# Second attention walks its keys from the back, spreads the score tiles for the maxima evenly, and masks them on VectorE and GpSimd instead of TensorE

## The chip, the cores and the metric

The kernel runs on one core of one Trainium2 chip. The metric is the device time of one execution in microseconds (us), the median of several runs. An engine is named as the profile names it: PE is TensorE (PEld its weight loads), DVE is VectorE, ACT is ScalarE, POOL is GpSimd, SP is SyncE.

## What is computed

Two transformer-like layers on x of shape (2, 1024, 128) in float32. Layer 0 is a latent attention with 8 heads and a mixture of experts. Layer 1, where the change is, is causal attention with 16 heads of width 8, then a second mixture of experts. The part that matters:

```
def _L1_attn_ref(x, w_qkv, w_out):
    qkv = x @ w_qkv
    q, k, v = jnp.split(qkv, 3, axis=-1)
    ...                                   # 16 heads of width 8, rotary embedding on q and k
    scores = jnp.einsum('bhqd,bhkd->bhqk', q, k) * scale
    causal = jnp.tril(jnp.ones((S, S), dtype=bool))
    scores = jnp.where(causal, scores, jnp.finfo(scores.dtype).min)
    attn = jax.nn.softmax(scores, axis=-1)
    out = jnp.einsum('bhqk,bhkd->bhqd', attn, v)
    out = out.transpose(0, 2, 1, 3).reshape(B, S, D)
    return out @ w_out
```

## The kernel before

Every engine has one program in order, written out by hand, and they wait for each other by semaphores. The second attention is cut into eight units (`U1 = 8`): a unit is one batch and four heads (`HG = 4`), with its 1024 queries in two chunks of 512 and its keys in eight tiles of 128.

Scores are computed twice. Once as queries x keys, in `scores_max1` (L1331), to find each query's maximum over its keys: 40 pieces a unit, listed in `MX1`, each of one or two matmuls (L1348) into one bank of PSUM, out of which DVE reduces the maximum in `maximum1` (L2021). On the diagonal a mask of large negative numbers is added by a further matmul of 128 columns for each tile (`mask_qk`, L1352). A second time as keys x queries, in `scores1` (L1374), with the maximum as an extra row of the operand: ten steps a unit (`K1 = 10`), listed in `ST1`, each of one key tile (or two that share a bank) for four heads in four banks. ACT takes the exponential in `exps1` (L851, two heads at a time), and `values1` (L1400) multiplies by the values. Here too the causal mask is a matmul of 128 columns (`masks1`, L1386), ahead of the exponential. All of these run through the same PE.

The maxima belong to the unit after: while PE runs the ten steps of unit u, it weaves in the 40 pieces of unit u+1, five in each of steps 0 to 7 and none in 8 and 9 (`MX1_STEP`, function `piece` in `unit1`). The pieces have two PSUM banks (0 and 1), so piece n waits until DVE has reduced piece n-2 (`max1_done`). In step k, `values1` of step k-1 is issued behind the scores and three of the pieces of step k. After the last piece DVE splits the maxima into two parts (`split_max1`), PE turns them (`turn_max1`, L1361), ACT copies them (`max_rows1`), and the next unit's `scores1` can begin. The stacked queries and keys of the units ahead are staged by POOL (`stage`), turned by PE (`turn_stack`, L1327) and copied by ACT (`stack`, L613) through bank 7, which the turned contexts (`turn_context1`, L1408, read by `contexts_out1` on DVE) share. Of unit 0 the 40 pieces run ahead of the units, among the preparation of the second batch, with six banks. Units 2 to 5 run in a hardware loop of two units.

The four score banks hold step k+1's scores once ACT has taken step k's exponentials (`exp1_done`).

## Time and profile before

| | |
|---|---|
| median of 3 runs | 993.67 us (993.42 to 994.7) |
| profiled execution | 993.18 us, span of its instructions 991.3 us |
| PE, PEld busy | 849.9 us (86%), 505.0 us (51%) |
| DVE, ACT, POOL busy | 595.4 (60%), 516.4 (52%), 329.3 us (33%) |
| second attention, maxima of unit 0 | 559 to 616 us of the span |
| second attention, the eight units | 621 to 939 us of the span |

Busy time is what an engine spent on instructions. A PE matmul's row lasts longer than the room it takes in PE's stream, since matmuls overlap: the room is read from one start to the next. "Idle before, releaser" tells what an engine waited for ahead of an instruction. PEclk is the clock that TensorE was granted, where 1.00 is 2.4 GHz.

### The profile page before, as it was taken

How to read it: one execution, taken by the hardware profiler on the slowest of the kernel's cores; microseconds unless marked ns; L12 is line 12 of the kernel's file. 1: busy time of each engine (PE TensorE's matmuls, PEld its weight loads, DVE VectorE, ACT ScalarE, POOL GpSimd, SP SyncE). 2: the span in 40 equal slices, each digit the busy share in tenths (PEclk: the TensorE clock that was granted, in tenths of full speed). 3: DMA queues.
4: the chain of work that ended last, by engine and by line, in shares of the span. 5: the costliest groups of instructions: out<-in, count | busy, mean ns of one | idle time of the engine just before them, and what ended most of it. 6: DMA issues, size and time to landing. Idle time of an engine off the chain costs nothing.

```text
span 991.3 us, 15069 instructions
## 1 busy us (share of the span) xinstructions
PE 849.9 (86%) x5146; PEld 505.0 (51%) x5146; DVE 595.4 (60%) x1294; ACT 516.4 (52%) x875; POOL 329.3 (33%) x332
## 2 busy tenths in 40 slices
PE   5899999988999865899998435899999999999858
PEld 2454444343343233479987323555555555555435
DVE  6867776767666157553357598557575575754051
ACT  3246566564565642336665211656656566565632
POOL 3327666655566861660140840110202102000000
PEclk9779999998999996799999566899999999999969
DMA  9300000000000000112230200000000000000001
GB/s 330 123 1 1 1 1 1 1 1 1 1 1 1 1 1 0 59 59 62 70 97 29 84 3 1 1 1 1 1 2 1 1 0 0 0 1 1 1 1 43
DMA packets 22634, 24.38 MB, mean 25 GB/s; under 512 B 3591, under 2 KB 20105, under 8 KB 22314
## 3 DMA queue, kind: packets, MB, share of 16 engines
q1 hardware_dynamic: 19896, 17.90, 5.5%
q0 software_dynamic: 2048, 4.20, 1.5%
q10 hardware_dynamic: 626, 1.43, 0.4%
q8 instruction: 40, 0.66, 0.3%
q14 instruction: 24, 0.20, 0.1%
HBM read 14.34 MB, written 9.18 MB: 24 GB/s over the span
## 4 chain that ended last, share of the span: by engine, by line
PE 62%; DVE 23%; ACT 7%; issue 5%; POOL 2%; DMA 1%; ACTq 0%; DVEq 0%; SPq 0%; POOLq 0%
PE ps L1348 8%; PE ps L1400 6%; PE ps L1032 6%; PE ps L1024 5%; PE ps L1001 5%; DVE mx_part L2021 5%; PE ps L1374 4%; DVE mx_part L1631 3%; ACT rounded L613 3%; PE ps L1040 3%; PE ps L1291 3%; DVE cT L1654 2%; PE ps L990 2%; PE ps L1202 2%; ACT pt L851 2%
## 5 line engine op out<-in xcount | busy, mean ns | idle before, releaser
L1631 DVE TENSOR_REDUCE mx_part<-ps 128x1 f32<-128x512 f32 x256 | 162.5, 681 | 70.6 <-PE ps L1001 69.8
L851 ACT ACTIVATE pt<-ps 128x1024 f32<-128x1024 f32 (+1 forms) x160 | 142.8, 938 | 86.7 <-PE ps L1374 45.7
L670 ACT ACTIVATE pt<-ps 128x512 f32<-128x512 f32 x256 | 139.9, 596 | 80.3 <-PE ps L1024 78.2
L2021 DVE TENSOR_REDUCE mx_part<-ps 128x1 f32<-128x512 f32 (+3 forms) x256 | 138.9, 586 | 37.7 <-PE ps L1352 23.9
L1348 PE MATMUL ps<-rounded 128*128 128x512 f32 (+3 forms) x384 | 143.1, 426 | 12.2 <-DVE mx_part L2021 4.5
L613 ACT ACTIVATE rounded<-ps 32x512 fp32r<-32x512 f32 (+3 forms) x166 | 98.2, 593 | 100.9 <-PE ps L1327 32.2
L1024 PE MATMUL ps<-rounded 100*128 100x512 f32 x256 | 121.0, 484 | 8.5 <-ACT pt L670 7.8
L1001 PE MATMUL ps<-rounded 98*128 98x512 f32 x256 | 107.9, 444 | 17.4 <-DVE mx_part L1631 16.7
L1348 PEld LDWEIGHTS ps<-rounded 128*128 128x128 f32 x384 | 73.7, 203 | 76.2 <-DVE mx_part L2021 49.8
L1374 PE MATMUL ps<-rounded 128*128 128x512 f32 (+3 forms) x384 | 104.2, 370 | 8.9 <-ACT pt L851 7.2
L2021 DVE TENSOR_REDUCE mx<-ps 128x1 f32<-128x128 f32 (+3 forms) x128 | 57.2, 487 | 83.4 <-PE ps L1352 82.0
L490 POOL TENSOR_TENSOR xnT<-pt 128x512 f32<-128x512 f32 x64 | 80.9, 1282 | 72.6 <-ACT pt L670 71.9
L490 POOL TENSOR_TENSOR xn<-pt 128x512 f32<-128x512 f32 x64 | 80.3, 1283 | 59.2 <-ACT pt L670 55.5
L1024 PEld LDWEIGHTS ps<-rounded 100*128 100x128 f32 x256 | 48.1, 191 | 78.8 <-ACT pt L670 46.7
L577 POOL COPY v_cur<-early 128x288 f32 (+1 forms) x8 | 3.4, 425 | 221.6 <-PE ps L1400 221.6
L1400 PE MATMUL ps<-pt,v_cur 128*9 128x512 f32 (+3 forms) x768 | 76.9, 488 | 0.1
L1032 PE MATMUL ps<-pt,ckv 128*32 128x512 f32 x512 | 74.8, 659 | 0.9 <-ACT pt L670 0.9
L1001 PEld LDWEIGHTS ps<-rounded 98*128 98x128 f32 x256 | 50.8, 201 | 47.7 <-issue 29.9
L1374 PEld LDWEIGHTS ps<-rounded 128*128 128x128 f32 x384 | 60.7, 191 | 24.0 <-ACT pt L851 17.0
L1987 DVE TENSOR_TENSOR pt<-ps,pt 128x352 f32<-128x352 f32 x46 | 24.1, 523 | 52.2 <-ACT pt L797 52.2
L1654 DVE RECIPROCAL cT<-ps 128x128 f32<-128x128 f32 x32 | 29.5, 936 | 39.1 <-PE ps L1040 39.1
L613 ACT ACTIVATE pt<-ps 128x128 f32<-128x128 f32 (+2 forms) x96 | 37.6, 393 | 25.6 <-PE ps L1283 14.4
(249 smaller groups left out, 1285.9 us busy)
## 6 DMA issues: line engine op xcount, KB each, us to landing
wm<-in_wm SPq DMA_DIRECT2D x1, 4896.0 KB, 15.5
kstage<-to_experts SPq DMA_DIRECT2D x10, 256.0 KB, 3.4
of_experts<-pt SPq DMA_DIRECT2D x10, 256.0 KB, 2.3
to_experts<-kstage SPq DMA_DIRECT2D x4, 512.0 KB, 4.1
wm<-in_experts SPq DMA_DIRECT2D x1, 1028.0 KB
x<-in_x SPq DMA_DIRECT2D x4, 256.0 KB, 6.2
out<-x SPq DMA_DIRECT2D x4, 256.0 KB, 2.3
to_experts<-kstage SPq DMA_DIRECT2D x2, 448.0 KB, 4.4
```

The costliest lines, as they stand in the source:

```text
L490: nc.gpsimd.tensor_tensor(pair_sum[j % 2][i], pt0(0, i), pt0(1, i), ALU.add).then_inc(pair_add, 1)
L613: return nc.scalar.activation(dst, src, ACT.Copy)
L670: nc.scalar.activation(pt0(k, i), ps[:, ST0_BANKS[i % 2], :], ACT.Exp, scale=SCALE0).then_inc(exp_done, 1)
L851: nc.scalar.activation(pt[:, 4 * (t % 2) + 2 * g:4 * (t % 2) + 2 * g + 2, 0:w], ps[:, ST1_BANKS[2 * g]:ST1_BANKS[2 * g] + 2, 0:w], ACT.Exp ...
L1001: mm(ps[:, max_bank(u, n), :], cq[0:NZ, b * S + j * P:b * S + (j + 1) * P], key_stack[u % 2][0:NZ, h, c * CH:(c + 1) * CH], start=True, st ...
L1024: mm(ps[:, ST0_BANKS[i % 2], :], key_stack[pp][0:NZM, h, k * P:(k + 1) * P], query_stack[pp][0:NZM, h, c * CH:(c + 1) * CH], start=True, s ...
L1032: ins = mm(ps[ctx_rows(pp, i), CTX_BANK, :], ckv[:, k, u // UH, :], pt0(k, i), start=(k == 0), stop=(k == TS - 1))
L1348: ins = mm(bank[:, o:o + w], query_stack1[pp][:, i * P:(i + 1) * P], key_stack1[pp][:, r, c * CH:c * CH + w], start=(o == 0), stop=not diag)
L1374: ins = mm(ps[:, ST1_BANKS[r], o:o + w], key_stack1[pp][:, r, j * P:(j + 1) * P], query_stack1[pp][:, q0:q0 + w], start=(o == 0), stop=not ...
L1400: ins = mm(ps[RS * r:RS * r + DH + 1, CTX_BANK, CH - w:CH], v_cur[pp][:, j, r, :], pt[:, 4 * (t % 2) + r, o:o + w], start=(j == 0), stop=( ...
L1631: v.tensor_reduce(mx_part[u % 2][:, o:o + 1], ps[:, max_bank(u, n), :], AX_X, ALU.max).then_inc(max_done, 1)
L2021: v.tensor_reduce(dst, ps[:, banks[s % len(banks)], o:o + w], AX_X, ALU.max).then_inc(max1_done, 1)
```

## The change

1. `ST1` is turned round: the second chunk of queries comes first, then the first, and in each the diagonal key tiles first and then the others from the back. `MX1` is turned round as well (second half of queries on the second half of keys, then on the first half, then the first half), with the pieces of one head side by side.
2. Four pieces in each of the ten steps, one behind each head's scores, in place of five in eight. The stream of pieces runs eight ahead (`MX1_AHEAD`): steps 8 and 9 of unit u hold the first eight pieces of unit u+2, and eight pieces of unit 1 stand ahead of unit 0.
3. No mask matmuls. For the maxima, DVE adds a mask tile `later` in SBUF and takes the maximum in one `tensor_tensor_reduce`, which writes the sum back to PSUM; it is two instructions on the engine. For the exponentials, POOL sets the forbidden ones to zero behind ACT (`mask`, `affine_select` on a block of 4 x 128 columns, eight blocks a unit), and `values1` of a diagonal step waits for POOL (`masked1`) in place of ACT.
4. The last step's values go into the next unit's step 0; the copies of keys by ACT are spread one by one behind the exponentials (`STACK1_KEYS`); POOL stages keys before queries, in separate functions; all eight units are written out, without the loop.

The core of the diff:

```
-for c in range(S // CH):
+for c in reversed(range(S // CH)):
     j0 = c * TC
-    ST1 += [(c, ((j, 0, CH),)) for j in range(j0 + 1)]
-    ST1 += [(c, ((j0 + 1, 0, CH - P), (j0 + 3, CH - P, P))), (c, ((j0 + 2, 0, CH - 2 * P),))]
+    own = [(c, ((j0, 0, CH),)), (c, ((j0 + 1, 0, CH - P), (j0 + 3, CH - P, P))), (c, ((j0 + 2, 0, CH - 2 * P),))]
+    ST1 += own + [(c, ((j, 0, CH),)) for j in reversed(range(j0))]
...
-    MX1 += [(r, c, p) for p in parts for r in range(HG)]
+    MX1 += [(r, c, p) for r in range(HG) for p in parts]
...
-MX1_STEP = (5, 5, 5, 5, 5, 5, 5, 5, 0, 0)
+MX1_AHEAD = 2 * HG
...
+            def mask(u, k):
+                if DIAG1[k]:
+                    pool.wait_ge(exp1_done, u * (2 * K1) + (2 * k + 2))
+                for o, w in DIAG1[k]:
+                    block = pt[:, 4 * (k % 2):4 * (k % 2) + HG, o:o + P]
+                    nc.gpsimd.affine_select(block, block, [[0, HG], [1, P]], ALU.is_ge, 0.0, base=0,
+                                            channel_multiplier=-1).then_inc(masked1, 1)
...
                 for i, o, w in parts:
-                    diag = c == i // TC
                     ins = mm(bank[:, o:o + w], query_stack1[pp][:, i * P:(i + 1) * P],
-                             key_stack1[pp][:, r, c * CH:c * CH + w], start=(o == 0), stop=not diag)
-                if diag:
-                    for i, o, w in parts:
-                        ins = mm(bank[:, o + w - P:o + w], identb[:], mask_qk[:], start=False,
-                                 stop=(o == parts[-1][1]))
+                             key_stack1[pp][:, r, c * CH:c * CH + w], start=(o == 0), stop=(o == parts[-1][1]))
...
-                pe.wait_ge(exp1_done, u * (2 * K1) + (2 * t + 2))
+                if DIAG1[t]:
+                    pe.wait_ge(masked1, u * NDIAG1 + DIAG1_UPTO[t])
+                else:
+                    pe.wait_ge(exp1_done, u * (2 * K1) + (2 * t + 2))
...
                 for k in range(K1):
-                    scores1(u, pp, 0, k, first)
-                    scores1(u, pp, 1, k, first)
-                    piece(k, 0)
-                    scores1(u, pp, 2, k, first)
-                    scores1(u, pp, 3, k, first)
-                    piece(k, 1)
-                    masks1(k)
-                    piece(k, 2)
+                    for r in range(HG):
+                        scores1(u, pp, r, k, first)
+                        piece(k, r)
...
+            for n in range(MX1_AHEAD):
+                scores_max1(1, 1, n)
+            for u in range(U1):
+                unit1(u, u % 2, first=(u == 0), s=(u + 1 < U1), t=(u + 2 < U1))
...
-                    v.tensor_reduce(dst, ps[:, banks[s % len(banks)], o:o + w], AX_X, ALU.max).then_inc(max1_done, 1)
+                    tile = ps[:, banks[s % len(banks)], o:o + w]
+                    if c == i // TC:
+                        v.tensor_tensor_reduce(tile, tile, later[:, CH - w:CH], 1.0, NEG, ALU.add, ALU.max,
+                                               dst).then_inc(max1_done, 1)
+                    else:
+                        v.tensor_reduce(dst, tile, AX_X, ALU.max).then_inc(max1_done, 1)
```

PE, steps 8 and 9 of a unit before, from the last head's scores of step 8 on. L1374 are scores, L1386 their masks, L1400 values, L1361 turned maxima; there is no piece in them:

```order
L1374 MATMUL ps<-rounded 128x384
L1374 MATMUL ps<-rounded 128x128
L1386 MATMUL ps<-mask_kq,identb 128x128 x8
L1400 MATMUL ps<-pt,v_cur 9x512 x4
L1361 MATMUL ps<-identr,qstage 128x128 x4
L1374 MATMUL ps<-rounded 128x256 x4
L1386 MATMUL ps<-mask_kq,identb 128x128 x4
L1400 MATMUL ps<-pt,v_cur 9x384 x4
L1400 MATMUL ps<-pt,v_cur 9x128 x4
L1361 MATMUL ps<-identr,qstage 128x128 x4
```

PE in step 8 now, from the second head on (L1403 are scores, L1382 pieces, L1420 values, L1428 turned contexts):

```order
L1403 MATMUL ps<-rounded 128x384
L1403 MATMUL ps<-rounded 128x128
L1382 MATMUL ps<-rounded 128x256
L1403 MATMUL ps<-rounded 128x384
L1403 MATMUL ps<-rounded 128x128
L1382 MATMUL ps<-rounded 128x512
L1403 MATMUL ps<-rounded 128x384
L1403 MATMUL ps<-rounded 128x128
L1382 MATMUL ps<-rounded 128x128
L1382 MATMUL ps<-rounded 128x384
L1420 MATMUL ps<-pt,v_cur 9x512 x4
L1428 MATMUL ps<-ident,cT 128x128 x4
```

What moved: the masks are gone, and a piece stands behind each head's scores.

DVE, a stretch of a unit before: one instruction for each tile, whether masked or not (register operations of the loop between them), and then a context:

```order
L2021 TENSOR_REDUCE mx_part<-ps 128x1
L2017 REGISTER_ALU
L2021 TENSOR_REDUCE mx_part<-ps 128x1
L2038 ISA
L2041 RECIPROCAL rden<-ps 128x16
L2042 ISA
L2045 ISA
L2045 TENSOR_TENSOR half<-ps,rden 128x4x32
```

DVE over the masked tiles of steps 7 to 9 now (ISA is the masked maximum and, behind it, the instruction that hands out its result):

```order
L2043 ISA ps,mx_part<-ps,later 128x128
L2043 ISA mx_part 128x1
L2043 ISA ps,mx_part<-ps,later 128x384
L2043 ISA mx_part 128x1
L2067 RECIPROCAL rden<-ps 128x16
L2071 TENSOR_TENSOR half<-ps,rden 128x4x32
L2043 ISA ps,mx_part<-ps,later 128x256
L2043 ISA mx_part 128x1
L2043 ISA ps,mx_part<-ps,later 128x512
L2043 ISA mx_part 128x1
```

What moved: a masked tile is a pair, and the masked tiles of the next unit but one stand on both sides of the context.

PE between the last piece of unit 0 and the scores of unit 0, before:

```order
L1361 MATMUL ps<-identr,qstage 128x128 x8
L1327 MATMUL ps<-identr,qstage 128x128 x4
L1327 MATMUL ps<-identr,kstage 128x128 x4
L1374 MATMUL ps<-rounded 128x512 x2
L1348 MATMUL ps<-rounded 128x128
L1348 MATMUL ps<-rounded 128x384
```

The same place now (L1391 turned maxima, L1363 turned stacks):

```order
L1391 MATMUL ps<-identr,qstage 128x128 x4
L1363 MATMUL ps<-identr,qstage 128x128 x4
L1391 MATMUL ps<-identr,qstage 128x128 x4
L1382 MATMUL ps<-rounded 128x128
L1382 MATMUL ps<-rounded 128x384
L1382 MATMUL ps<-rounded 128x256
L1382 MATMUL ps<-rounded 128x512
...
L1403 MATMUL ps<-rounded 128x512
```

What moved: three groups of transposes in place of four, and eight pieces that stood in unit 0's steps before.

## Rows read from the trace of the kernel before

**Rows 1.** The page: busy times, and the chain that ended last.
```profile
PE 849.9 (86%) x5146; PEld 505.0 (51%) x5146; DVE 595.4 (60%) x1294; ACT 516.4 (52%) x875; POOL 329.3 (33%) x332
...
PE 62%; DVE 23%; ACT 7%; issue 5%; POOL 2%; DMA 1%; ACTq 0%; DVEq 0%; SPq 0%; POOLq 0%
```

**Rows 2.** Timeline, POOL: start us, us, instruction; the copy that ends each unit.
```profile
666.20 0.42 POOL L577 COPY v_cur<-early 128x288 f32 x1 [42.34 <-PE ps L1400]
...
748.57 0.42 POOL L577 COPY v_cur<-early 128x288 f32 x1 [35.80 <-PE ps L1400]
...
872.48 0.43 POOL L577 COPY v_cur<-early 128x288 f32 x1 [35.98 <-PE ps L1400]
```

**Rows 3.** Windows (start:end, length, busy PE, PEld, DVE, ACT, POOL, clock, DMA): one unit; unit 0's maxima.
```profile
748.58:789.87 41.29, 39.16 (x289) 23.39 (x289) 25.97 (x55) 26.00 (x35) 5.00 (x11) 1.00 0.01 1
...
560.00:585.00 25.00, 10.86 (x41) 7.54 (x41) 23.61 (x56) 0.60 (x1) 18.23 (x22) 0.57 0.09 24
```

**Rows 4.** Waits in that unit: who waited for whom, us, times, longest.
```profile
PEld ps L1348 <- DVE mx_part L2021: 7.2, 12, 1.0
...
PEld ps L1348 <- DVE mx L2021: 1.4, 3, 0.9
```

**Rows 5.** Timeline, PE, in and around that unit.
```profile
742.18 0.62 PE L1386 MATMUL ps<-mask_kq,identb 128*128 128x128 bf16 x8
742.73 1.05 PE L1400 MATMUL ps<-pt,v_cur 128*9 128x512 f32 x8
...
761.26 0.71 PE L1374 MATMUL ps<-rounded 128*128 128x512 f32 x2
...
765.04 0.63 PE L1374 MATMUL ps<-rounded 128*128 128x512 f32 x2
...
782.31 1.33 PE L1374 MATMUL ps<-rounded 128*128 128x384 f32 x8
```

**Rows 6.** Groups by form: busy, mean ns.
```profile
L2021 DVE TENSOR_REDUCE mx_part<-ps 128x1 f32<-128x512 f32 x160 | 103.8, 686 | 21.6 <-PE ps L1348 13.2 <-PE ps L1352 8.2
...
L1352 PE MATMUL ps<-mask_qk,identb 128*128 128x128 bf16 x256 | 50.1, 238 | 0.0
...
L1386 PE MATMUL ps<-mask_kq,identb 128*128 128x128 bf16 x256 | 22.6, 221 | 0.0
...
L2021 DVE TENSOR_REDUCE mx_part<-ps 128x1 f32<-128x128 f32 x32 | 9.2, 286 | 7.5 <-PE ps L1352 7.2
```

**Rows 7.** Timeline, DVE: short instructions, free ones and two that depend.
```profile
592.55 0.37 DVE L1929 BATCH_NORM_AGGREGATE mv<-stats 128x2 f32<-128x6 f32 x4
...
593.84 0.16 DVE L1947 TENSOR_TENSOR norm<-norm 128x4 f32<-128x4 f32 x1
594.03 0.16 DVE L1949 SCALAR_TENSOR_TENSOR norm<-norm 128x4 f32<-128x4 f32 x1
```

**Rows 8.** Groups by form: an addition on DVE from PSUM and SBUF, and one from two of SBUF.
```profile
L1918 DVE SCALAR_TENSOR_TENSOR x<-xnT,share,x 128x128 f32<-128x128 f32 x32 | 8.7, 346 | 0.0
...
L1749 DVE TENSOR_TENSOR x<-ps,x 128x512 f32<-128x512 f32 x4 | 2.7, 674 | 0.0
```

**Rows 9.** Groups of POOL and ACT.
```profile
L490 POOL TENSOR_TENSOR xnT<-pt 128x512 f32<-128x512 f32 x64 | 80.9, 1282 | 72.6 <-ACT pt L670 71.9
...
L468 POOL TENSOR_SCALAR xn<-x,mv,lnv 128x128 f32<-128x128 f32 x8 | 6.3, 789 | 1.4 <-DVE lnv L1579 1.4
...
L566 POOL COPY xn<-big 128x256 f32 x12 | 4.8, 400 | 39.3 <-PE ps L1361 38.0 <-POOL kstage L574 1.0
```

**Rows 10.** Timeline, PE: first pieces of unit 0, the turned maxima, first scores, and unit 7's.
```profile
558.96 0.90 PE L1348 MATMUL ps<-rounded 128*128 128x128 f32 x2 [2.48 <-ACT rounded L613]
...
616.41 0.75 PE L1361 MATMUL ps<-identr,qstage 128*128 128x128 f32 x4 [6.47 <-DVE qstage L2034]
...
621.40 1.18 PE L1374 MATMUL ps<-rounded 128*128 128x512 f32 x2
...
911.82 1.21 PE L1374 MATMUL ps<-rounded 128*128 128x512 f32 x4
```

More of the change, by code:

```diff
@@ L125 @@
 MX1 = []
-for i0, c in ((0, 0), (TC, 0), (TC, 1)):
+for i0, c in ((TC, 1), (TC, 0), (0, 0)):
     if c * TC == i0:
@@ new lines, in exps1 @@
+            def exps1(u, t, g, first):
+                w = sum(m for _, _, m in ST1[t][1])
+                act.wait_ge(st1_mm, u * (2 * K1) + (2 * t + g + 1))
+                if not (first and t < 2):
+                    act.wait_ge(pv1_mm, u * K1 + (t - 1))
+                nc.scalar.activation(pt[:, 4 * (t % 2) + 2 * g:4 * (t % 2) + 2 * g + 2, 0:w],
+                                     ps[:, ST1_BANKS[2 * g]:ST1_BANKS[2 * g] + 2, 0:w], ACT.Exp,
+                                     scale=SCALE1).then_inc(exp1_done, 1)
@@ L874, in _ @@
+                    if k == 0 and not first:
+                        context1_T(u - 1, 1)
+                    if k == K1_FIRST:
+                        context1_T(u, 0)
             act.wait_ge(keys_zero[0], 1)
-            for n in range(4):
-                stack(0, 0, n)
+            for n in range(2):
+                for r in range(HG):
+                    stack_keys(0, 0, n, r)
+                stack_queries(0, 0, n)
             for c in range(NCH // B, NCH):
@@ L1426, in unit1 @@
                     if k:
                         values1(u, pp, k - 1, first)
-                    for n in range(3, max(MX1_STEP)):
-                        piece(k, n)
-                    if s and k in STACK1_SECOND:
-                        n = 2 + STACK1_SECOND.index(k)
-                        turn_stack(u + 1, 1 - pp, n, (stacked, u * 4 + (n + 4)))
-                    if k == CTX1_BEFORE and not first:
-                        turn_context1(u - 1, 1, (stacked, u * 4 + 8) if s else (m1_rows, u * 2 + 2))
@@ L2072, in _ @@
             split_max1(0, 0)
-            unit1(0, 0, first=True)
-            unit1(1, 1)
-            with dve.Fori(1, U1 // 2 - 1) as i:
-                unit1(i * 2, 0)
-                unit1(i * 2 + 1, 1)
-            unit1(U1 - 2, 0)
-            unit1(U1 - 1, 1, s=False)
+            for n in range(MX1_AHEAD):
+                maximum1(1, 1, n)
+            for u in range(U1):
+                unit1(u, u % 2, s=(u + 1 < U1), t=(u + 2 < U1))
             contexts_out1(U1 - 1, 1)
```

324 lines of the change are left out of this document (169 added, 155 removed).

## The prediction, made before the changed kernel was run

> **What bounds the kernel now.** I read the page first. PE is busy for 86% of the span, holds 62% of the chain that ended last, and DVE holds 23% of it [rows 1]. That is an average over stages, so the next view is the stage that the change touches. The copy of the values by POOL stands at the end of each unit; from 666.20 to 872.48 us there are five units of 41.3 us each [rows 2]. The windows show one of them: in 41.29 us PE is busy for 39.16, DVE for 25.97 and ACT for 26.00, at a full clock of 1.00 [rows 3]. So the five units, unit 6 (872.48 to 911.82, 39.3 us) and unit 7 (about 26.8 us, without pieces) [rows 2, 10] are PE's.
>
> PE's 39.16 us are not all work. A matmul that waits for a semaphore also shows its weight load late, and the waits say that the loads of the pieces stood for 7.2 + 1.4 us behind DVE's maxima in that unit [rows 4]. The two banks of the pieces tie PE to DVE: five pieces in a step are some 3.3 us for DVE at 0.69 us each [rows 6], and a step without any mask takes 3.78 us (761.26 to 765.04) [rows 5]. Steps 8 and 9, in which DVE has nothing, take 7.6 us (782.31 to the end of the unit at 789.87) [rows 3, 5].
>
> The stage ahead is another one. While the maxima of unit 0 are taken, DVE is busy for 23.61 of 25 us and PE for 10.86, at a granted clock of 0.57, near the lower of its two levels (1.2 of 2.4 GHz) [rows 3]. There DVE is the bound, from the first pieces at 558.96 to the split maxima at 616.41 [rows 10].
>
> **The masks that PE loses.** 256 + 256 mask matmuls [rows 6] are 64 a unit. Their rows of 0.22 to 0.24 us overlap; eight in a line took from 742.18 to 742.73, 0.069 us each [rows 5]. That is 64 x 0.069 = 4.4 us of PE's stream a unit, and 41.3 - 4.4 = 36.9 us if every wait stays as it is. It can be less: a mask in front of a wait for DVE only filled that wait.
>
> **What DVE gets.** A unit has 32 masked tiles (four heads, two diagonal chunks, four tiles each), and on each the reduction becomes an addition with maximum and a second instruction. A reduction costs 0.286 us for 128 columns and 0.686 for 512, so 1.04 ns a column and 0.15 us fixed [rows 6]. An addition of PSUM and SBUF of 512 columns took 0.674 us [rows 8], so the first of the pair costs no more than the reduction did, if it runs a column at a time. The trace has no such pair. For the second, the nearest rows are short instructions on a few columns: free ones start 0.07 us apart ((0.37 - 0.16) / 3), dependent ones 0.19 [rows 7]. I take 0.09, near the free ones, as nothing stands between the two, and keep 0.05 to 0.25. DVE then has 25.97 + 32 x 0.09 = 28.9 us a unit (27.6 to 34). Four masked pieces are 4/3 of a head's 1.94 + 4 x 0.09 = 2.30, so 3.1 us a step; four plain ones 2.7 us.
>
> The Trainium skill, "VectorE: DVE Perf Modes", section on two Vector instructions with no wait between them, says that an operation which writes out its accumulator is two instructions, and that one is held until all earlier ones end only if its start quadrants differ. Here all start in partition 0, so by the page the second is not held; the free rows 0.07 us apart agree.
>
> **Four pieces in every step.** The plain step of 3.78 us loses one piece, some 0.35 us, to 3.4. Ten such are 34 us, and the turned tiles (eight groups of four a unit, some 0.37 us of room each) bring 2.9: 36.9 us again. Two short steps of 256 columns take off 0.8. Against it stand the waits which the new order makes. In step 8 the turned context must be read by DVE before the turned maxima may use the bank: DVE waits for PE there, 0.5 us. The split of the maxima stands behind the last piece of step 7, three dependent instructions, 0.6 us, ahead of step 8's pieces. Together 37.2 us a unit with the POOL wait below at nothing; DVE's 3.1 us in masked steps hide behind the 3.4. I keep 35.0 to 40.0.
>
> **POOL's masks.** Eight blocks of 4 x 128 columns a unit, one in four steps and two in two. The values of step k stand behind the scores and pieces of step k+1, so that after the second exponential PE still has two heads' scores and two pieces, about 1.6 us, ahead of them. No row shows the operation. A copy of 256 columns took 0.400 us, an addition of 512 took 1.282, and an operation with two scalars of 128 columns 0.789 [rows 9]: for 512 columns 0.8, 1.3 and 3.2 us. I take the middle, 1.3 us or less: one block is covered, two (2.6 us) are late by up to 1 us, in which DVE works off its two banks. POOL has time: 5.00 us busy in 41.29 [rows 3]. Its own staging of keys comes ahead of the mask of step 0, 2.4 us of the 3.2 before that exponential ends.
>
> **ACT** keeps its 26.00 us [rows 3]; with a context and two copies in step 0 it has 3.7 us there, once, covered by the scores' banks. Its exponentials in diagonal steps start earlier by PE's masks.
>
> **The start.** DVE-bound, so 32 pairs cost 32 x 0.09 = 2.9 us. Keys are staged, turned and copied before queries, which lets the first piece start 1.8 us earlier. Then eight pieces of unit 1 (two thirds of a unit's 2.30 x 4, 6.1 us for DVE) stand on PE ahead of the first scores: 616.41 moves to 617.5, three groups of transposes as close as before end near 621, the last piece is issued about 5 us later, scores at 626 instead of 621.40 [rows 10]. Unit 0 took 44.8 us from there to 666.20 [rows 2, 10], with stalls at its start that are now gone. With 37.2 + 1 for the table of the exponential it ends at 664.4: 1.8 us won, start and unit 0 together.
>
> **The sum.** Units 1 to 5: 5 x (41.3 - 37.2) = 20.5. Start and unit 0: 1.8. Unit 6 has no pieces in steps 8 and 9, 37.2 - 1.8 = 35.4 against 39.3: 3.9. Unit 7: 12 + 12 + 8 masks less on PE, but its values now wait for POOL with no pieces for cover: nothing, within 3 us. Unrolling: nothing; the other stages are written out as well. Total 26.2 us. The profiled execution took 993.18 us, 1.9 more than its span, and 0.5 less than the median: 993.7 - 26.2 = 967.5, so 968 us.
>
> **Rivals.**
>
> *PE's masks had filled waits.* For it: the pieces' 8.6 us behind DVE [rows 4]. Against it: in steps 8 and 9 no piece is there to wait. Only the 32 masks of the scores would count (2.2 us) less what new waits cost (0.9), so 40 us a unit: 7 x 1.3 less 1 at the start, about 985 us.
>
> *The spread frees more.* If the 8.6 us behind DVE shrink by half, a unit is 35.0 us, near PE's own work: 6 x 2.2 + 3 more than forecast, about 952 us.
>
> *The masked maximum takes two cycles a column (slower).* It reads and writes the same bank of PSUM column by column, which no row of before does. 10,240 masked columns a unit x 1.04 ns = 10.7 us on DVE: 39.6 us, plus its waits for contexts and split and the gap behind the values, 2.5 to 4, is 43 us. DVE is then the bound: 7 x 43 against 7 x 41.3, with the start (DVE-bound, 10.7 + 2.9 and the eight pieces 9 us) about +30, 1023 us. It decides from 26.2 / 256 = 0.10 us more for each of the 8 x 32 masked tiles than I take, if all of it lands on the path. Against it: 0.674 us for 512 columns of an addition that reads PSUM and writes elsewhere [rows 8].
>
> The Trainium skill, "Vector Engine (DVE) Microarchitecture Reference", section on points that are easy to get wrong, states that the scalar-tensor-tensor form with two sources in SBUF that are not bf16 halves throughput. Here one source is PSUM, so by the page it does not apply; the trace's own addition of that form from two float32 tiles of SBUF, 0.346 us for 128 columns [rows 8], shows no doubling either, without an accumulator.
>
> *POOL's masks are slow (slower).* At 2.5 us a block, single blocks are 0.9 us late and double ones 3.4: 4 x 0.9 + 2 x 3.4 = 10.4 us a unit on PE, less 3 of slack: 44.6 us, about 1025 us. It decides from 1.7 us a block.
>
> **How the numbers follow.** Forecast 0.42 (959 to 977), filled waits 0.17, more freed 0.13, the costs and gains cancel 0.05, slow maximum 0.13, slow POOL 0.10. Faster by over 0.2% (2 us, what this measurement can tell): 0.72. Same: 0.05. Slower: 0.23. The range reaches to the rival of 952 below, and above to 1004, beyond the upper bound of the second instruction: 0.16 us more on 256 tiles are 41 us, less 0.3 us of slack in six steps of seven units, 12.6, which gives 996: some 0.06 lie below and 0.14 above.
>
> **What would show it.** Units 37.2 us apart by the copies of the values; DVE busy 28 to 30 us in each, the pair's second instruction under 0.1 us from start to start; POOL's block at 1.3 us or less, with the values waiting for it only after the double blocks; DVE idle in no step for more than 1.5 us; first scores near 626 us, at the start. It is wrong if DVE has no idle time in masked steps, if values wait for POOL in single ones, or if the clock of 1.00 in the units falls as PE waits more.

## The result, and the profile after

| | before | changed |
|---|---|---|
| median of the runs | 993.54 us (4 runs) | 949.74 us (947.73 to 950.35, 4 runs) |
| ratio, 95% interval | | 0.9554, 0.9537 to 0.9571 |
| span of the profiled execution | 991.3 us | 948.6 us |

The kernel is 4.5% faster. The forecast was 968 us, 2.6% faster, in a range from 951 to 1004: the direction held, the gain was 44 us instead of 26, and the time fell 1.3 us below the range.

Page of the changed kernel, busy times and chain, against [rows 1]:

```profile
PE 814.8 (86%) x4634; PEld 478.3 (50%) x4634; DVE 605.9 (64%) x1550; ACT 518.4 (55%) x875; POOL 368.2 (39%) x396
...
PE 62%; DVE 27%; ACT 5%; issue 4%; POOL 2%; DMA 1%; ACTq 0%; SPq 0%; DVEq 0%; POOLq 0%
```

PE lost its 512 mask matmuls and 35 us of busy time. The shares of the chain hardly moved: which engine holds it says nothing of how much shorter it is. Timeline of POOL, the copies that mark the units, against [rows 2]:

```profile
706.55 0.43 POOL L588 COPY v_cur<-early 128x288 f32<-128x288 f32 x1
742.70 0.43 POOL L588 COPY v_cur<-early 128x288 f32<-128x288 f32 x1
```

A unit takes 36.15 us instead of 41.3. Its window and its waits, against [rows 3, 4]:

```profile
706.55:742.70 36.15, 34.74 (x226) 19.65 (x224) 27.77 (x88) 26.23 (x35) 9.95 (x20) 1.00 0.00 1
```

```profile
DVE ps L2043 <- PE ps L1382: 4.4, 8, 1.1
...
DVE mx_part L2046 <- PE ps L1382: 2.2, 3, 0.9
PEld ps L1382 <- DVE mx_part L2046: 2.2, 6, 0.5
PEld ps L1382 <- DVE mx L2043: 1.8, 4, 0.7
```

PE's busy time fell from 39.16 to 34.74, by 4.42 us, which looks like the 64 x 0.069 us of the prediction but isn't the masks alone (see e18 and e19); its idle time fell from 2.13 to 1.41. The pieces' weight loads wait for DVE for 5.0 us in all (a third row of 1.0 us, for the masked partial maxima, beside the two shown) instead of 8.6, and DVE itself waits 6.6 us for pieces.

Where the 42.7 us of span went, by the starts of the units' scores in both traces:

| stretch | before | after | won | forecast |
|---|---|---|---|---|
| start to first scores, and unit 0 | 621.40 + 44.8 | 621.27 + 36.6 | 8.3 | 1.8 |
| units 1 to 5 | 5 x 41.3 | 5 x 36.13 | 25.8 | 20.5 |
| unit 6 | 39.3 | 33.7 | 5.6 | 3.9 |
| unit 7 | 27.4 | 25.2 | 2.2 | 0 |
| behind it | 52.0 | 51.2 | 0.9 | 0 |

The first row is a sum of four: the start stage begins 1.6 us later in the trace of the changed kernel (its memset on DVE at 547.07 instead of 545.46 us), is 6.5 us shorter, is followed by 4.7 us more between the split maxima and the first scores, and unit 0 is 8.2 us shorter.

### The profile page after: what moved, and what is told of

The parts are those of the page before. It is cut to its first block, busy times and chain, and to the rows that moved or that the text cites. A ratio compares the mean times of both kernels' runs of the same rounds, so it can differ in the third digit from the quotient of the medians.

```text
span 948.6 us, 13753 instructions
## 1 busy us (share of the span) xinstructions
PE 814.8 (86%) x4634; PEld 478.3 (50%) x4634; DVE 605.9 (64%) x1550; ACT 518.4 (55%) x875; POOL 368.2 (39%) x396
## 4 chain that ended last, share of the span: by engine, by line
PE 62%; DVE 27%; ACT 5%; issue 4%; POOL 2%; DMA 1%; ACTq 0%; SPq 0%; DVEq 0%; POOLq 0%
PE ps L1382 7%; PE ps L1420 6%; PE ps L1068 6%; PE ps L1060 6%; DVE ps L2043 5%; PE ps L1403 5%; PE ps L1037 5%; DVE mx_part L1651 4%; PE ps L1076 3%; PE ps L1327 3%; DVE cT L1674 2%; PE ps L1238 2%; ACT rounded L645 2%; PE ps L1026 2%; PE ps L1309 2%
## 5 line engine op out<-in xcount | busy, mean ns | idle before, releaser
L1651 DVE TENSOR_REDUCE mx_part<-ps 128x1 f32<-128x512 f32 x256 | 162.4, 681 | 70.4 <-PE ps L1037 69.6
L882 ACT ACTIVATE pt<-ps 128x1024 f32<-128x1024 f32 (+1 forms) x160 | 148.9, 938 | 65.2 <-PE ps L1403 63.8
L1382 PE MATMUL ps<-rounded 128*128 128x512 f32 (+3 forms) x384 | 140.6, 410 | 11.6 <-DVE mx L2043 4.8
L2043 DVE CUSTOM_DVE_ANT_0 ps<-ps,later 128x128 f32<-128x128 f32 (+3 forms) x256 | 119.4, 519 | 45.6 <-PE ps L1382 44.8
L1060 PE MATMUL ps<-rounded 100*128 100x512 f32 x256 | 123.3, 493 | 8.5 <-ACT pt L702 7.9
L1403 PE MATMUL ps<-rounded 128*128 128x512 f32 (+3 forms) x384 | 124.0, 367 | 0.6 <-ACT pt L882 0.2
L1037 PE MATMUL ps<-rounded 98*128 98x512 f32 x256 | 106.0, 433 | 18.2 <-DVE mx_part L1651 17.3
L597 POOL TENSOR_SCALAR_AFFINE_SELECT pt<-pt 128x512 f32<-128x512 f32 x64 | 40.0, 637 | 207.9 <-ACT pt L882 207.9
L1382 PEld LDWEIGHTS ps<-rounded 128*128 128x128 f32 x384 | 74.2, 203 | 49.7 <-DVE mx L2043 15.5
L2046 DVE TENSOR_REDUCE mx_part<-ps 128x1 f32<-128x512 f32 x128 | 82.0, 686 | 16.3 <-PE ps L1382 16.0
L1403 PEld LDWEIGHTS ps<-rounded 128*128 128x128 f32 x384 | 69.4, 190 | 45.1 <-issue 21.2
L1060 PEld LDWEIGHTS ps<-rounded 100*128 100x128 f32 x256 | 49.3, 196 | 81.6 <-ACT pt L702 45.8
L1420 PE MATMUL ps<-pt,v_cur 128*9 128x512 f32 (+3 forms) x768 | 76.8, 488 | 1.5 <-POOL pt L597 1.5
L548 POOL DMA_INDIRECT xnT<-of_experts,slot_i x32 | 30.7, 960 | 57.1 <-DMA of_experts<-pt 47.8
```

Source lines behind the costliest of these rows:

```text
L882: nc.scalar.activation(pt[:, 4 * (t % 2) + 2 * g:4 * (t % 2) + 2 * g + 2, 0:w], ps[:, ST1_BANKS[2 * g]:ST1_BANKS[2 * g] + 2, 0:w], ACT.Exp ...
L1037: mm(ps[:, max_bank(u, n), :], cq[0:NZ, b * S + j * P:b * S + (j + 1) * P], key_stack[u % 2][0:NZ, h, c * CH:(c + 1) * CH], start=True, st ...
L1060: mm(ps[:, ST0_BANKS[i % 2], :], key_stack[pp][0:NZM, h, k * P:(k + 1) * P], query_stack[pp][0:NZM, h, c * CH:(c + 1) * CH], start=True, s ...
L1382: ins = mm(bank[:, o:o + w], query_stack1[pp][:, i * P:(i + 1) * P], key_stack1[pp][:, r, c * CH:c * CH + w], start=(o == 0), stop=(o == p ...
L1403: ins = mm(ps[:, ST1_BANKS[r], o:o + w], key_stack1[pp][:, r, j * P:(j + 1) * P], query_stack1[pp][:, q0:q0 + w], start=(o == 0), stop=(o ...
L1420: ins = mm(ps[RS * r:RS * r + DH + 1, CTX_BANK, CH - w:CH], v_cur[pp][:, j, r, :], pt[:, 4 * (t % 2) + r, o:o + w], start=(j == CTX1_START ...
```

## The experiments

Every ratio is to the kernel before, run on the same chip. Two groups of runs (e10 to e13, and e18 with e19; marked *) fell on chips on which the kernel before took 1034 us; in their traces the start stage begins 35 to 41 us later than in the others. Units are as long there as elsewhere (compare e10 with the changed kernel, e12 with e1). So most verdicts are read from the distance of two copies that mark a unit, which repeats within 0.1 us in one trace from unit 2 on, and from the way between two DVE instructions of the start stage: its memset and the first instruction of the split maxima. "Start" is that distance: 70.45 us before, 63.95 after. The starts marked * can't be compared with the others: in each of them DVE stands for 3 to 9 us in all at places where no trace of the other chips has waits of that length, whether the run moves the zeroing on GpSimd (e10 to e12) or not (e13, e18, e19). Why is open, and the kernel before has no trace from these chips.

| run | us | ratio (95%) | unit | start |
|---|---|---|---|---|
| changed kernel | 949.7 | 0.9554 (0.9537 to 0.9571) | 36.13 | 63.95 |
| e1 plain maxima | 942.8 | 0.9482 (0.9458 to 0.9507) | 35.37 | 63.1 |
| e3 one-column memset more | 948.4 | 0.9565 (0.9540 to 0.9589) | 36.12 | 63.9 |
| e13 96-column memset more | 1001.7 | 0.9708 (0.9664 to 0.9751) | 36.80 | 72.1* |
| e2 no GpSimd masks | 950.8 | 0.9568 (0.9541 to 0.9595) | 36.13 | 64.2 |
| e7 GpSimd's masks twice as long | 960.0 | 0.9668 (0.9640 to 0.9695) | 36.94 | 63.9 |
| e4 maxima's masks on PE | 964.5 | 0.9699 (0.9666 to 0.9731) | 37.12 | 69.2 |
| e17 scores' masks on PE | 956.8 | 0.9633 (0.9607 to 0.9660) | 37.08 | 64.0 |
| e18 both on PE | 1017.9 | 0.9840 (0.9804 to 0.9876) | 39.05 | 71.9* |
| e19 both, and five pieces | 1023.7 | 0.9906 (0.9871 to 0.9942) | 40.74 | 70.9* |
| e5 five pieces | 959.3 | 0.9665 (0.9632 to 0.9698) | 37.85 | 64.0 |
| e6 before, maxima's masks on DVE | 983.2 | 0.9910 (0.9880 to 0.9939) | 39.98 | 70.5 |
| e8 values in halves | 1022.7 | 1.0303 (1.0269 to 1.0337) | 45.00 | 64.0 |
| e10 zeroing late | 991.1 | 0.9611 (0.9565 to 0.9657) | 36.11 | 67.8* |
| e12 the same, plain maxima | 982.7 | 0.9526 (0.9483 to 0.9569) | 35.37 | 64.9* |
| e11 before, zeroing late | 1035.6 | 1.0031 (1.0002 to 1.0059) | 41.28 | 71.3* |
| e14 zeroing between | 948.9 | 0.9537 (0.9511 to 0.9563) | 36.13 | 61.3 |
| e15 before, zeroing between | 985.9 | 0.9918 (0.9891 to 0.9946) | 41.29 | 62.8 |
| e16 zeroing between, plain maxima | 939.9 | 0.9465 (0.9441 to 0.9488) | 35.38 | 60.3 |

### What the masked maximum costs: e1, e3, e13

DVE's timeline of the changed kernel, unit 0's first maxima:

```profile
559.48 0.60 DVE L2043 CUSTOM_DVE_ANT_0 ps<-ps,later 128x384 f32<-128x384 f32 x1
560.00 0.14 DVE L2043 DVE_READ_ACCUMULATOR2_ANT mx_part<- 128x1 f32 x1
560.00 0.47 DVE L2043 CUSTOM_DVE_ANT_0 ps<-ps,later 128x256 f32<-128x256 f32 x1
560.38 0.14 DVE L2043 DVE_READ_ACCUMULATOR2_ANT mx_part<- 128x1 f32 x1
560.38 0.73 DVE L2043 CUSTOM_DVE_ANT_0 ps<-ps,later 128x512 f32<-128x512 f32 x1
561.03 0.14 DVE L2043 DVE_READ_ACCUMULATOR2_ANT mx_part<- 128x1 f32 x1
561.03 0.33 DVE L2043 CUSTOM_DVE_ANT_0 ps<-ps,later 128x128 f32<-128x128 f32 x1
```

Read the starts, not the durations: the accumulator's read and the next main instruction start together. The four tiles of a head start 0.52 + 0.38 + 0.65 us and, from 561.03 to the next row, 0.25 us apart: 1.79 us a head.

```
- v.tensor_tensor_reduce(tile, tile, later[...], 1.0, NEG, ALU.add, ALU.max, dst)
+ v.tensor_reduce(dst, tile, AX_X, ALU.max)                       # e1
+ v.memset(x_lo[:, n:n + 1], 0.0)            # e3, behind each masked maximum
+ dve.wait_ge(max1_done, done); v.memset(x_lo[:, slot:slot + 96], 0.0)  # e13, the same place
```

> The changed kernel, with a plain maximum over the unmasked scores in place of the masked maximum in all 256 own-half tiles (32 in a unit; the causal mask of the maxima is left out). Theory A: the masked maximum costs no more than a plain one, since its second instruction (the read of the accumulator) lies under the start of the next one; then the time stays within 1.5 us of the changed kernel's 949.7 us. Rival B, the price of the prediction: 0.09 us for each second instruction, 2.9 us of VectorE a unit, of which TensorE waits for a part; then the time falls to between 930 and 945 us.

> The changed kernel with one more small VectorE instruction (a memset of one column, 128x1) behind each of the 256 masked maxima, which brings back the 0.09 us that the prediction charged for the second instruction, or somewhat less. VectorE gets 1.9 to 2.9 us a unit more. Theory A: VectorE stands idle for about 1 us in each step, at the values, and TensorE waits for it in the rest of the step, so that a third to a half comes through: 0.7 to 1.4 us a unit, 956 to 961 us. Rival B: all of it comes through, as VectorE is the bound within masked steps: 965 to 972 us. Rival C: the idle time takes it all: under 952 us.

> The changed kernel with a memset of 96 columns on VectorE behind each of the 256 masked maxima (some 0.08 us more of VectorE's stream each, by its memset of 4096 columns in 3.47 us, plus what it can't overlap), close to the 0.09 us of the prediction's step. With plain maxima 0.055 us less on 32 tiles gave 0.77 us a unit, so that 44% of VectorE's time came through. Theory A: the same share of 2.6 us: units 1.1 us longer, 37.3 us, and 2.5 us in the start stage: 960 us (956 to 963). Rival B: hidden like the memset of one column: 950 to 952. Rival C: all of it: units of 38.7 us, 970 us.

e1 gave 0.76 us a unit (and 0.9 in the start). Theory A, a pair no dearer than a plain maximum, falls by 5 us; 942.8 lies in B's band, but B's reason falls too, since the read has no time of its own in the rows above. Plain maxima of four tiles take 1.63 us back to back: e15 has 12 of them in one row.

```profile
561.02 4.88 DVE L2022 TENSOR_REDUCE mx<-ps 128x1 f32<-128x128 f32 x12 [11.20 <-PE ps L1353]
```

4.88 / 3 = 1.63 against 1.79: the main instruction costs 0.04 us a tile more than the reduction, 1.3 us a unit, the read nothing. Of these 1.3 us more than half (0.76) came through to the unit. The read is in time what the Trainium skill, "VectorE: DVE Perf Modes", section on two Vector instructions with no wait between them, calls not held; the prediction quoted it and still charged 0.09. A small instruction more (e3, rival C) costs nothing either: the unit stays at 36.12 us and the start at 63.9. e13's memset, which also has a wait on a semaphore ahead of it (for the tile before), does cost:

```profile
759.74 0.14 DVE L2048 MEMSET x_lo<- 128x96 f32 x1
759.80 0.54 DVE L2043 CUSTOM_DVE_ANT_0 ps<-ps,later 128x384 f32<-128x384 f32 x1
760.25 0.14 DVE L2043 DVE_READ_ACCUMULATOR2_ANT mx<- 128x1 f32 x1
760.35 0.14 DVE L2048 MEMSET x_lo<- 128x96 f32 x1
760.40 0.41 DVE L2043 CUSTOM_DVE_ANT_0 ps<-ps,later 128x256 f32<-128x256 f32 x1
```

A head now takes 759.43 to 761.75, 2.32 us, so memset and wait take 0.13 us more a tile and 4.2 us a unit; the unit became 0.67 us longer. One sixth came through, where A had said 44%; DVE's idle time in the unit fell from 8.4 to 6.5 us. By this run the predicted 0.09 us would have cost about 0.67 x 0.09 / 0.13 = 0.46 us a unit, an estimate; why e1 let through more than half and e13 a sixth is open. e13's total can't be read against the changed kernel's, since its start stage has a stand of its chip in it.

### What GpSimd's masks cost: e2, e7

```
- nc.gpsimd.affine_select(block, block, ...)         # e2: none
+ nc.gpsimd.affine_select(idle, idle, ...)           # e7: one more, ahead of each
```

> The changed kernel without the 64 instructions of GpSimd on the exponentials (the causal mask of the exponentials is left out); the values wait for the exponentials themselves. Theory A: the masks are hidden in units 0 to 6, and cost only the 1.5 us by which the values wait for GpSimd in unit 7: 948 us, between 947 and 949.5. Rival B: they also hold buffers and so hold back ScalarE and TensorE in every unit: under 945 us.

> The changed kernel with a second, idle GpSimd instruction of the same form and size ahead of each of the 64 masks of exponentials, so that a block takes about 1.3 us (the price that the prediction took) instead of 0.64, and a step with two blocks 2.5 us. Theory A: single blocks stay hidden, double blocks come up to 1 us late in each unit's two steps, at most 2 us a unit, and unit 7 pays 2 to 3 us: 953 to 966 us. Rival B: hidden in all units but the last: 951 to 953 us. Rival C: GpSimd becomes the bound with its staging behind the masks: over 970 us.

Groups by form of the changed kernel (busy us, mean ns), and two PE rows of unit 7:

```profile
L597 POOL TENSOR_SCALAR_AFFINE_SELECT pt<-pt 128x512 f32<-128x512 f32 x64 | 40.0, 637 | 207.9 <-ACT pt L882 207.9
```

```profile
878.58 1.05 PE L1420 MATMUL ps<-pt,v_cur 128*9 128x384 f32 x16 [0.79 <-POOL pt L597]
...
895.14 1.55 PE L1420 MATMUL ps<-pt,v_cur 128*9 128x384 f32 x24 [0.71 <-POOL pt L597]
```

A block is 0.64 us, half of the 1.3 taken. Without the masks (e2, whose exponentials stay unmasked) units are as long as with them; theory B falls, and the 1.5 us of unit 7 that the trace shows can't be told in the total (950.8, above theory A's 949.5). At 1.27 us a block (e7) a unit is 0.81 us longer. From values to values its steps are those of the changed kernel but for the two with double blocks, 0.3 and 0.5 us longer: single blocks stay hidden at the predicted price, double ones come up to 0.5 us late. The step of the prediction on POOL's cover held, and theory A; its price was double.

### What each part of the change is worth in a unit: e4, e17, e18, e5, e19, e6

```
+ mm(bank[:, o + w - P:o + w], identb[:], mask_qk[:], start=False, ...)     # e4, e18, e19
+ mm(ps[:, ST1_BANKS[r], o:o + P], identb[:], mask_kq[:], start=False, ...) # e17, e18, e19
- MX1_AHEAD = 2 * HG; piece n = HG * k + r + MX1_AHEAD
+ MX1_AHEAD = 0; five pieces in steps 0 to 7                                # e5, e19
```

> The changed kernel with the maxima's masks back on TensorE: 32 mask matmuls a unit and plain maxima; everything else (order, four pieces a step, GpSimd's masks of the exponentials) stays. Theory A: each mask matmul takes its 0.069 us of TensorE's stream, 2.2 us a unit, less the 0.77 us that plain maxima gave: units of 37.6 us instead of 36.13, 960 us in all (957 to 963). Rival B: the matmuls fill waits for VectorE: units under 36.7 us, 951 to 954 us.

> The changed kernel with the pieces spread as before: five in each of the steps 0 to 7 (the fifth behind the values), none in 8 and 9, and none ahead of a unit; no other change. Theory A: the spreading was worth what the waits for VectorE lost, 8.6 us of weight loads before against 5.0 after, of which the idle time of TensorE shows 0.7 us: units of 36.9 us, and the eight pieces ahead of unit 0's scores come back into the unit: 953 to 958 us. Rival B: all 3.6 us of the waits return: units near 39.7 us, 970 to 978 us. Rival C: the spread is worth nothing, units of 36.1 us, and the time is 948 to 951.

> The kernel before, with only the maxima's masks moved: masked maxima on VectorE, no mask matmuls in the 32 masked tiles of a unit (VectorE's program is unrolled for it); the masks of the scores stay on TensorE, five pieces a step. Theory A: TensorE loses 2.2 us a unit and the pair costs 0.8: units of 39.5 to 39.9 us instead of 41.3, 981 to 985 us. Rival B: the masks had filled waits for VectorE, which is slower now: 41.0 us or more, 991 us or above. Rival C: with the masks gone, waits shrink with them: under 39 us, below 978.

> The changed kernel with the masks of the scores back on TensorE (32 mask matmuls a unit, each behind its head's scores) and none by GpSimd. Theory A: they cost their stream, 32 x 0.055 to 0.069: units of 37.9 to 38.3 us instead of 36.13, and the parts add up: 36.13 + 2.0 + 1.0 (maxima's masks) + 1.7 (spread) = 40.8 of the 41.3 before; ratio to before 0.970. Rival B: they add more, 3 us a unit or above, since they lengthen ScalarE's way in the masked steps too: 0.977 or above. Rival C: under 1 us a unit: then the rest is the order's (keys from the back, copies by head).

> The changed kernel with both kinds of masks back on TensorE (64 mask matmuls a unit) and four pieces a step. Theory A: a mask alone fills waits for VectorE, two kinds do so less: more than the sum of the single runs, 36.13 + 2.5 to 3.5 = 38.6 to 39.6 us a unit. Rival B: they add up: 38.1 us a unit.

> As the run beside it, and with five pieces in steps 0 to 7 and none in 8 and 9: all that is left of the change is the order (keys from the back, maxima by head, copies by head, the places of the turned tiles) and the unrolling. Theory A: the order is worth nothing in a unit: 41.0 to 41.5 us, as before. Rival B: the order is worth the missing 1.5 us: 39.8 us a unit or less.

POOL's copies in e4, e17, e18, e19 and e5, each in its fence:

```profile
754.22 0.43 POOL L588 COPY v_cur<-early 128x288 f32<-128x288 f32 x1
791.37 0.42 POOL L588 COPY v_cur<-early 128x288 f32<-128x288 f32 x1
```

```profile
743.43 0.42 POOL L589 COPY v_cur<-early 128x288 f32<-128x288 f32 x1
780.51 0.42 POOL L589 COPY v_cur<-early 128x288 f32<-128x288 f32 x1
```

```profile
760.08 0.42 POOL L589 COPY v_cur<-early 128x288 f32<-128x288 f32 x1
799.11 0.43 POOL L589 COPY v_cur<-early 128x288 f32<-128x288 f32 x1
```

```profile
755.24 0.42 POOL L589 COPY v_cur<-early 128x288 f32<-128x288 f32 x1
795.96 0.42 POOL L589 COPY v_cur<-early 128x288 f32<-128x288 f32 x1
```

```profile
741.00 0.42 POOL L588 COPY v_cur<-early 128x288 f32<-128x288 f32 x1
778.83 0.43 POOL L588 COPY v_cur<-early 128x288 f32<-128x288 f32 x1
```

Undone one after the other from the changed kernel, the parts are worth: both kinds of masks 36.13 to 39.05 (2.9 us), the spread on top 39.05 to 40.74 (1.7), the order and unrolling that are left 40.74 to 41.3 (0.6). So 5.2 us are accounted for in full. With five pieces a step the masks are worth the same (e19 to e5, 40.74 to 37.85). Theory A of e19 (41.0 to 41.5) is missed by 0.3, B falls.

PE's busy time in a unit tells another sum. Windows of e18, e19 and e5:

```profile
760.08:799.11 39.03, 38.73 (x289) 22.84 (x289) 26.45 (x56) 26.50 (x35) 5.01 (x11) 1.00 0.01 2
```

```profile
755.24:795.96 40.72, 39.76 (x289) 22.90 (x288) 26.30 (x56) 26.39 (x35) 5.00 (x12) 1.00 0.00 1
```

```profile
741.00:778.83 37.83, 35.44 (x224) 19.37 (x224) 27.77 (x89) 26.32 (x35) 9.91 (x19) 1.00 0.00 1
```

The masks take 4.0 us of it at four pieces a step (38.73 to 34.74) and 4.3 at five (39.76 to 35.44), but a unit gets only 2.9 us shorter: PE's idle time grows by 1.1 and 1.4 us as they leave.

The two kinds of masks do not add up. Either kind alone costs 1.0 us (e4, e17), both 2.9 (e18: theory A), where their stream is 4.4. In e4 and e18 plain maxima give back e1's 0.76 us, so that the masks themselves cost 1.75 us of 2.2 in e4 and 3.7 of 4.4 in e18. The rest went into waits: the weight loads of the pieces stand for DVE for 5.0 us in a unit of the changed kernel, 3.8 in e17, 2.5 in e4 (4.1 in e1) and 2.6 in e18. So either kind fills waits for DVE, and behind the maxima's masks the others find no more of them. e17 meets its rival C (under 1 us a unit) by 0.05 us, its total lies between A and C, and what C concludes, that the rest is the order's, falls by e18 and e19. e4 lies between its theories A and B in a unit and came to 964.5 us by its start, below. The rival "PE's masks had filled waits" was right by a third. e6 agrees: from before, moving the maxima's masks alone gave 1.3 us of the 2.2 of their stream (theory A).

Waits of the pieces' weight loads in a unit of e5, then of e18:

```profile
PEld ps L1382 <- DVE mx L2040: 4.4, 7, 0.9
PEld ps L1382 <- DVE mx_part L2040: 3.6, 8, 0.9
PEld ps L1382 <- DVE mx_part L2043: 3.5, 9, 0.7
```

```profile
PEld ps L1380 <- DVE mx_part L2045: 2.2, 5, 0.5
PEld ps L1380 <- DVE mx L2045: 0.4, 1, 0.4
```

e5 shows the spread's 1.7 us in a unit, twice its theory A, with and without the masks (e19 against e18). These waits are what it takes away: 11.5 us in e5 against 5.0 with four pieces, 7.9 in e19 against 2.6. Its start is shorter by the eight pieces (first marking copy at 665.27 instead of 670.44), so the total lost 9.6 us and not 12.

### Values in halves: e8

```
- values1(k - 1), all heads, behind the fourth piece
+ values1(k - 1, heads 0, 1) behind the third, (heads 2, 3) behind the fourth
```

> The changed kernel with the values of a step in two halves (heads 0 and 1 behind the third piece, heads 2 and 3 behind the fourth) instead of one block behind the fourth, to close the 0.6 to 1.1 us in which VectorE has no piece in each step. Theory A: VectorE gets its pieces evenly, the 5.0 us for which TensorE's weight loads wait for it in a unit shrink to 2 or 3, and TensorE's idle 1.4 us go to 0.7: units of 35.4 us, 944 us (942 to 947). Rival B: TensorE's own stream is the bound and its idle time is elsewhere: no change, 948 to 951. Rival C: the first half waits for ScalarE or GpSimd, having one head of scores and a piece less ahead of it: units over 36.5 us, 953 us or more.

The time is 73 us longer. It lies in rival C's open band (953 us or more), but not for its reason: in a unit the values' weight loads wait 0.2 us for ScalarE and never for GpSimd. All three theories fall. Timeline of PE in e8, then in the changed kernel:

```profile
693.63 1.03 PE L1421 MATMUL ps<-pt,v_cur 128*9 128x512 f32 x4
694.59 0.50 PE L1403 MATMUL ps<-rounded 128*128 128x512 f32 x1
```

```profile
710.64 1.05 PE L1420 MATMUL ps<-pt,v_cur 128*9 128x512 f32 x8
711.61 0.50 PE L1403 MATMUL ps<-rounded 128*128 128x512 f32 x1
```

Eight matmuls of four heads and four matmuls of two heads hold PE for 0.97 and 0.96 us until the next scores start: the four heads, whose results go to four separate quarters of the partitions, run side by side, and half of them take as long as all. In each of the ten steps the second half costs what the whole did, 0.97 us, or 0.55 in the two steps of 256 columns: 8.9 us, and a unit grew by 8.87.

### The start stage: e10, e11, e12, then e14, e15, e16

Timeline of DVE and POOL in the start stage, of the kernel before, then of the changed one:

```profile
570.08 3.53 POOL L593 MEMSET rounded<- 128x4096 f32 x1
...
570.98 4.43 DVE L1927 COPY norm<-stats 128x4 f32<-128x4 f32 x1
...
577.38 0.65 DVE L1947 TENSOR_TENSOR norm<-norm 128x4 f32<-128x4 f32 x1
```

```profile
571.68 3.53 POOL L614 MEMSET rounded<- 128x4096 f32 x1
...
572.73 5.03 DVE L1978 TENSOR_SCALAR xn<-x,mv,norm 128x128 f32<-128x128 f32 x4
```

Before, the norm's chain of small instructions begins beside POOL's memsets: its head stands for 4.4 us until they end, and those behind it run beside POOL's staging at 0.16 to 0.65 us each. After, the chain is done 3 us earlier against POOL's clock and only its last step meets the memsets. e4 puts the masks back, its first mix comes 0.8 us later, and the whole collision returns (start 69.2 us). The first try moved the memsets behind the chain, the second ahead of it:

```
+ pool.wait_ge(max1_done, MX1_END[SECOND_ADD[0] + 1])   # e10, e11, e12: ahead of the memsets
- gather(1); memsets
+ first half of gather(1); memsets; second half           # e14, e15, e16
```

> The changed kernel with GpSimd's zeroing of unit 1's tiles in the start stage held until VectorE has taken the first maximum behind the first mix. In the changed kernel the copy of the normalized rows (VectorE) took 5.03 us beside these memsets and 1.12 us in its second place. Theory A: VectorE's copy cannot run beside GpSimd's memsets; free of them it gives back up to 3.9 us: from VectorE's own memset to the split maxima 60.0 us instead of 63.9, 946 us in all (944 to 948). Rival B: what holds the copy is something else (its own data): 949 to 951. Rival C: the memsets now collide with the second mix or hold up the staging of unit 1, and nothing is won or up to 3 us lost.

> The kernel before with the same delay of GpSimd's zeroing. There the blocked instruction is the copy at the head of the norm's chain (4.43 us instead of 0.17), and the 12 small instructions behind it ran beside GpSimd's staging (0.16 to 0.65 us each). Theory A: both go: 4.1 and about 3 us, from VectorE's memset to the split maxima 63.5 us instead of 70.45: 986 us (984 to 988), and half of what the change won in the start stage was that its chain of small instructions came ahead of the memsets. Rival B: only the blocked copy: 989 us. Rival C: no change, 993.

> The changed kernel with plain maxima (the causal mask of the maxima left out) and with GpSimd's zeroing held as in the run beside it. Theory A: the two gains are in different places (0.77 us a unit, and 3.9 us in the start stage) and add up: 939 us (937 to 941). Rival B: in the start stage they overlap: 942 to 943.

In e10, e11 and e12 the memsets lay beside plain maxima and cost nothing, but POOL's staging behind them (619.93 to 625.35 us in e10) met the second mix (as rival C of e10 had it):

```profile
620.20 4.86 DVE L1939 SCALAR_TENSOR_TENSOR x<-xnT,share,x 128x128 f32<-128x128 f32 x8
```

It takes 2.18 us undisturbed. The Trainium skill, "SBUF — State Buffer", section on its two separate sides, has a rule that sorts these rows: GpSimd shares a port pair, one at a time, with DVE instructions in a two-port mode, and with those that have two sources in SBUF only where GpSimd's instruction reads SBUF. The traces agree: a copy of one source stood beside a memset (4.43 us), a mix of two sources beside copies and additions (4.86), and reductions from PSUM beside neither. That the copy ran in a two-port mode no row shows.

The distances of e10 and e11 (67.8 and 71.3 us) hold the stands of their chip ahead of the norm, as in e10's first mix:

```profile
604.45 0.35 DVE L1939 SCALAR_TENSOR_TENSOR x<-xnT,share,x 128x128 f32<-128x128 f32 x1 [0.80 <-DVE x L1939]
```

Behind them, from the norm's first instruction to the split maxima, e10 takes 40.8 us where the changed kernel takes 42.4, and e11 40.3 where the kernel before takes 45.8. So the late zeroing gave 1.6 and 5.5 us there, with the second mix's 2.7 and 2.8 us already taken off, less than theories A had said (3.9 and 7); the totals show no gain (0.9611, 1.0031). In e12 the stands (up to 0.9 us, 3.4 in all) lie between the norm's small instructions, and its total shows no gain over e1 either. e18 has e4's start stage, and there the stands put the norm behind the memsets: from its first instruction to the split 39.9 us instead of e4's 46.8.

> The changed kernel with GpSimd's zeroing of unit 1's tiles put between the two halves of its gather, 10 us earlier, where VectorE only takes maxima out of PSUM. Theory A: VectorE's copy of the normalized rows (5.03 us beside the memsets, 1.12 alone) comes free, and maxima from PSUM are not held by memsets: from VectorE's memset to the split maxima 60 us instead of 63.9, and 4 us less in all, a ratio to before of 0.951. Rival B: masked maxima, which read one source from SBUF, are held by the memsets in turn: no gain. Rival C: the second half of the gather is 5.4 us later and the second mix waits for it: up to 3 us lost.

> The kernel before with the same move of GpSimd's zeroing. Theory A: the head of the norm's chain loses its 4.3 us, and the small instructions behind it, now ahead of GpSimd's staging, most of their stretch (12 of them took 0.16 to 0.65 us each, about 2.7 us too much): from VectorE's memset to the split maxima 63.5 to 66 us instead of 70.45, ratio to before 0.993 to 0.996. Then some 3 us of what the change won in the start stage was a change of place against GpSimd. Rival B: no change, the chain is held by something else.

> The changed kernel with plain maxima (the causal mask of the maxima left out) and the zeroing between the halves of the gather: the likely best of both. Theory A: 0.77 us a unit, 0.9 and 4 us in the start stage: 938 to 940 us where the kernel before takes 993, a ratio of 0.945. Rival B: the start gives nothing more, 0.949.

Timeline of DVE in e15, memset and split, then the chain's head:

```profile
546.35 3.47 DVE L2012 MEMSET rounded<- 128x4096 f32 x1 [0.92 <-DVE big L1976]
...
571.87 0.17 DVE L1928 COPY norm<-stats 128x4 f32<-128x4 f32 x1
...
609.35 0.22 DVE L2035 SCALAR_TENSOR_TENSOR qstage<-mx,qstage 128x32 fp32r<-128x32 f32 x1
```

The head takes 0.17 us instead of 4.43, and the start of the kernel before is 7.7 us shorter (62.8 us), more than theory A gave. With the changed kernel the same move gives 2.7 us (61.3), under theory A's 4 and not to be told in the total (948.9): its copy takes 1.22 us, but the second mix (3.52 us) now meets POOL's staging. In a start stage free of the memsets the change is thus worth 1.5 us; the other 5.0 of its 6.5 are the change of place. Masked maxima (one source in SBUF) beside POOL's memsets keep their 0.60 and 0.73 us in e14, so its rival B falls.

e16 is the fastest of all runs: 939.9 us, 0.9465 of before and 10 us under the changed kernel, as its theory A had it. It leaves the mask out of the maxima only, which are the shift of the exponentials; the shift divides out as long as a masked score doesn't lie so far above the visible ones that these vanish, and that depends on the data.

## Why the prediction was right or wrong

**Right.** PE was the bound in the units. The masked maximum runs a column at a time: 0.25 us for 128 and 0.65 for 512 columns, so the rival of two cycles falls. POOL's single blocks are hidden even at the price that I took. The eight pieces ahead of the first scores cost near what was said: 6.3 us from the last transposes to the scores instead of 5.

**Wrong, the masks' worth.** "64 x 0.069 = 4.4 us of PE's stream a unit, and 41.3 - 4.4 = 36.9 us if every wait stays as it is": the stream was right, but the waits did not stay. The masks were worth 2.9 us of a unit. That PE's busy time fell by 4.42 us is luck: the masks took 4.0 to 4.3 of it, the spread 0.7 to 1.0, and the order added 0.6.

**Wrong, the step "Four pieces in every step".** "Together 37.2": 36.13 came out. I gave the spread its room but no gain, and added 1.1 us of new waits; of these PE's stand for the turned context was 0.2 us. In a unit the forecast was 4.4 for the masks less 0.3 for all else; the runs gave 2.9 for the masks, 1.7 for the spread and 0.6 for the order. Two errors of 1.5 and 2.0 us nearly cancelled, and the order's 0.6 had stood at nothing. Together they are the 5.3 us missed in units 1 to 5 and the 1.7 of unit 6. This is the rival "the spread frees more", to which I gave 0.13, half of the way to its 35.0.

**Wrong, the pair's second instruction.** "For the second ... I take 0.09": it is 0, and the main instruction 0.04 us dearer. In a unit the forecast had hidden all of DVE's time behind PE's, so this price was no part of 37.2. In the start it stood with 2.9 us, where e1 shows 0.9.

**Wrong, the start.** The sum had the split maxima 1.1 us later ("616.41 moves to 617.5"); against the memset they came 6.5 us earlier. The stage is bound by DVE, but by when its instructions meet POOL's: 5.0 of these 7.6 us are the collision that e15 takes out of the kernel before, 2.0 the pair, 0.6 stay open. Beyond the split, the way to the first scores was 1.2 us longer than said and unit 0's gain 1.8 us larger, and the stage began 1.6 us later, which leaves the 6.5 us missed in the table. The collision's rows stood in the trace of before (4.43 us for a copy of four columns), and I didn't read them.

**Unit 7** gave 2.2 us and not nothing: its masks left PE, and its values waited 1.5 us for POOL.

All misses but that of the masks have one sign: each cost that no row showed was taken in the middle, and each gain without a row at nothing.

## What to carry to other kernels

Two engines that are tied by two banks gain from an even supply, and it pays to price this by itself: here it gave 1.7 of 5.2 us, with the masks and without them. Busy time that leaves an engine is not time that leaves the path: 4.0 us of matmuls gave 2.9 us, and their two halves, undone one at a time, 1.0 each. Look for instructions far above the time of their neighbours of the same form in the trace of before: an instruction of four columns at 4.4 us is a collision, and a shift of 0.8 us can set it off or end it. Before a group of matmuls is cut up, see whether its parts run side by side: the time of the group is not the sum of its parts.
